# Depthwise taps as 64x64 matmuls, raw token rows, and norms after the gather, in a convolution and expert-choice kernel

## The chip, the cores and the metric

The kernel runs on one core of a Trainium2 chip. The core has a matrix engine (PE, with its weight loads shown apart as PEld), a vector engine (DVE), an activation engine (ACT), a general engine (POOL), a queue engine (SP), and 16 DMA engines. Each engine takes its instructions in order and waits on semaphores. The metric is the device time of one execution in microseconds: median 534.0 of three runs, 533.0 to 535.27. Below, "us" is microseconds and a line number such as L691 is a line of the kernel before.

## The reference

The input is 16 images of 128 channels and 28 x 28 positions. Two blocks follow each other, each added to its input.

```
h = LN over channels(x)                              # per position
h = relu(bn1(depthwise 3x3(h) + b)); a channel whose largest |h| is below 4.0 becomes 0
h = relu(bn2(pointwise 128x128(h) + b)); a channel whose largest |h| is below 0.001 becomes 0
x1 = x + h
t  = x1 as 12544 token rows of 128
n  = LN over a row(t)
logits = n @ Wr (8 experts); probs = softmax over all tokens
per expert: the 1024 tokens of largest prob; gelu(n[idx] @ W1 + b1) @ W2 + b2, times the prob
out = x1 + the sum of these rows, added at their tokens
```

## The kernel before, in words

**Stage 1, the images (until about 213 us).** `step(pair, u)` of each engine is one beat. In beat k the engines work on images k, k-1, ..., k-5 at once (`image(pair, u, lag)`); the middle of the beats is a hardware loop, the first and last are written out. For one image, in order:

- SP loads x. PE turns it (`turn_x`, L704, 7 transposes of 112 positions) into PSUM `psA`; DVE takes `bn_stats` of each token (L964), and a few small operations (`moments_a/b/c`, `inverse`, `shift`) with a square root on ACT (L463) between them make scale and shift. ACT norms the 7 tiles into `ln_tok` (L538), PE turns them back into `psB` (L769), and ACT copies them into the zero-padded `x_pad` (L570).
- The depthwise taps: PE does four of the nine, with a diagonal 128x128 weight each (`conv_half`, L691): two halves of 14 lines (392 columns), each half in a bank of its own of `psC`. DVE adds the other five: `first_tap` reads `psC` per half, then four `later_tap` over all 784 columns (L1009).
- ACT applies bn1 and relu (L519) and counts signs (L509). DVE turns the count into a 0/1 per channel and masks the pointwise weights (`mask_weights`, L1085). PE multiplies (L729), ACT applies bn2 and relu (L492) and counts signs (L500), DVE adds the masked result to x (`residual_sum`, L1103): this is x1, copied to `x1_all` by DMA.
- PE turns x1 into token rows in `psD` (L746) and computes the logits beside them (L750, 14 instructions). DVE takes the rows' statistics (L964), then the scaled logits (L1118, L1121). ACT norms the 7 tiles of 112 x 128 into `rows` (`norm_rows`, L483), and SP stores them in `token_rows`, 136 floats a token.

**Stage 2, the search (213 to 259 us).** DVE, ACT and PE find each expert's threshold in 16 rounds.

**Stage 3, the experts (259 to 462 us).** For each expert DVE finds the slots of its tokens (`slots_a` to `slots_d`, the index `slot_idx`). POOL gathers 1024 rows in 8 indirect DMAs (L403) and later adds the results to DRAM in 8 (L423, L426); `gather` and `scatter` of different experts stand in a fixed order on POOL. PE turns the gathered rows (`turn_picked`, L836), ACT copies them, PE does W1 (L857), ACT the gelu (L633), PE does W2 (L869), DVE adds the bias (L1302) and weighs (L1310). While the last expert runs, the sums of the first four experts are loaded, turned (`turn_first`, L923) and added to `x1_all` (`add_first`, L1343).

**Stage 4 (to the end).** The late sums are loaded, turned (L945), added and stored.

**The order by hand.** Every engine's order within a beat is written out. `turn_picked` waits only for its gather's DMA (L834). On DVE, `slots_*` of expert e+3 stand ahead of the bias and weighing of expert e.

Of the kernel before, what the change touches and what calls it, by code (L numbers as in the profile page):

```python
# [12 lines left out]
ds = bass.ds  # L13
# [11 lines left out]
ROW = C + E  # L25
# [3 lines left out]
HS = CAP // 2  # L29
DW_THRESH, PW_THRESH = 4.0, 0.001  # L30
# [5 lines left out]
PE_TAPS = 4  # L36
# [4 lines left out]
LOOP_FIRST, LOOP_END, LAST_PAIR = 3, B // 2 - 1, B // 2 + 3  # L41
# [37 lines left out]
def build(nc, x, dw_w, dw_b, bn1_g, bn1_b, bn1_m, bn1_v, pw_w, pw_b, bn2_g, bn2_b, bn2_m, bn2_v,  # L79
# [6 lines left out]
    with ExitStack() as ctx:  # L86
# [36 lines left out]
        zero_rows = sb("zero_rows", [P, TPI * C])  # L123
# [4 lines left out]
        tap_diag = sb("tap_diag", [128, PE_TAPS, 128])  # L128
# [72 lines left out]
        hid = sb("hid", [128, FT, CAP])  # L201
        y_sum = sb("y_sum", [128, SB, C])
# [13 lines left out]
        def ln_region(img):  # L216

            return row_tiles if isinstance(img, int) and img in (1, 3) else ln_tiles

        last_tiles = psC[0:P, :, :].rearrange("p a (t c) -> p (a t) c", c=C)  # L220

        def row_region(img):
            if isinstance(img, int) and img == B - 1:
                return last_tiles
            return ln_tiles if isinstance(img, int) and img == B - 3 else row_tiles
# [4 lines left out]
        def logit_region(img):  # L230
            return row_region(img)[:, TPI, 0:TPI * E].rearrange("p (t e) -> p t e", e=E)
# [14 lines left out]
        s_x1c = pair_of("x1_kept")  # L246
        s_t3, s_m3, s_std3, s_n3, s_rl = (sem(n) for n in (
            "row_tokens", "row_stats", "row_std", "row_normed", "row_logits"))
# [23 lines left out]
        s_pool, s_act = sem("pool_past_waits"), sem("act_past_waits")  # L272
# [9 lines left out]
        def _(sp):  # L282
# [6 lines left out]
            sp.dma_start(taps_w[:, :], dw_w.rearrange("c a h w -> c (a h w)")).then_inc(s_prm, 16)  # L289
            load_x(1, 1)  # L290

            def step(pair, u):
                on, img, q, use = image(pair, u, -2)
                if on:
                    sp.wait_ge(s_t1, img * 2 - 2)
                    load_x(img, q)
                on, img, q, use = image(pair, u, 2)
                if on:
# [3 lines left out]
                    if isinstance(img, int) and img == 0:  # L302
                        sp.wait_ge(s_const, 1)
                    sp.dma_start(y_t[:, ds(img, 1), :, :].rearrange("p i t c -> p (i t) c"),
                                 zero_rows[:, :].rearrange("p (t c) -> p t c", c=C)).then_inc(s_yz, 16)
                on, img, q, use = image(pair, u, 5)
                if on:
                    sp.wait_ge(s_rl, img + 1)
                    sp.wait_ge(s_n3, img + 1)
                    sp.dma_start(rows_t[:, ds(img, 1), :, :].rearrange("p i t c -> p (i t) c"),  # L310
                                 rows[:, q, :].rearrange("p (t c) -> p t c", c=ROW)).then_inc(s_rows[q], 16)
                on, img, q, use = image(pair, u, 3)
                if on:
                    sp.wait_ge(s_x1, img + 1)
                    sp.dma_start(x1_all[:, ds(img * HW, HW)], x1[:, q, :]).then_inc(s_x1c[q], 16)
# [12 lines left out]
            for img in range(B):  # L328
                sp.dma_start(late_t[:, ds(img, 1), :, :].rearrange("p i t c -> p (i t) c"),
                             zero_rows[:, :].rearrange("p (t c) -> p t c", c=C)).then_inc(s_lz, 16)  # L330
# [35 lines left out]
        def _(pool):  # L366
# [14 lines left out]
            nc.gpsimd.memset(zero_rows[:, :], 0.0)  # L381
# [73 lines left out]
        def _(act):  # L455
# [6 lines left out]
            def ln_root(img):  # L462
                nc.scalar.activation(ln_sm[:, 4, :], ln_sm[:, 3, :], ACT.Sqrt, bias=eps_c[0:P, :],  # L463
                                     scale=1.0 / C).then_inc(s_std1, 1)

            act.wait_ge(s_mom, 1)
            ln_root(0)
            act.wait_ge(s_bnv, 1)
            nc.scalar.activation(fold[:, 2:4], fold[:, 0:2], ACT.Sqrt).then_inc(s_bns, 1)

            def step(pair, u):
                onN, imgN, _, _ = image(pair, u, -1)
# [3 lines left out]
                on, img, q, use = image(pair, u, 0)  # L476

                def norm_rows():
                    act.wait_ge(s_sc, img5 + 6)
# [5 lines left out]
                    ins.then_inc(s_n3, 1)  # L485

                def second_activation():
# [9 lines left out]
                    if on2 and since(img2, 1):  # L497
                        act.wait_ge(s_sg1, img2)
# [4 lines left out]
                def first_signs():  # L503
                    if since(img2, 1):
                        act.wait_ge(s_kp1, img2)
                    if on3:
                        act.wait_ge(s_sg2, img3 + 1)
                    act.wait_ge(s_h1, img2 + 1)
# [14 lines left out]
                if ending and on3:  # L523
                    second_activation()
# [3 lines left out]
                if on5:  # L528
                    norm_rows()
# [868 lines left out]
```

## Time and profile before

| what | value |
|---|---|
| runs | 535.27, 533.0, 534.0 us; median 534.0 |
| span of the profiled execution | 502.9 us, 6936 instructions |
| median less span (what lies around the span) | 31.1 us |
| busy over the span | PE 361.9 us (72%), PEld 255.7 (51%), DVE 327.1 (65%), ACT 274.3 (55%), POOL 159.3 (32%) |
| granted TensorE clock, mean | 0.857 of full speed |

The profiled execution's time is told by its span, first to last instruction; what lies around it is taken as the difference to the median of the runs. Busy times are sums over the whole span, and the four stages have different limits. A row of the page's "busy tenths" shows this at a glance: each digit is one fortieth of the span (12.6 us).

```profile
PE   4989888888889985631021798999990498876575
DVE  5699988888889898578879548556620025235444
ACT  3577888888888876677640528556551240510000
POOL 4000000000000000000005777787888788876000
```

### The profile page before, as it was taken

Reading aid. Unit: us, or ns where it says so; the run is one execution under the profiler, and the core shown is the slowest. Engines: PE = TensorE matmul, PEld = TensorE weight load, DVE = VectorE, ACT = ScalarE, POOL = GpSimd, SP = SyncE. Lnnn points to the kernel's source line nnn. Section 1 sums busy time; section 2 is a strip of 40 time slices with the busy share of each in tenths; the row PEclk is TensorE's granted clock in tenths of the full one; section 3 lists DMA queues with packets and bytes.
Section 4 is the critical chain, followed back from the end, with each engine's and each line's share of the span. In section 5 each row is a group of like instructions: output and inputs, shape, how many; then the busy total and the mean of one; then the engine's idle time right before and its main releaser. Section 6 shows DMA issues by size and latency. Waiting matters only on the chain. (4 is left out here: it accounts for less than half of the span.)

```text
span 502.9 us, 6936 instructions
## 1 busy us (share of the span) xinstructions
PE 361.9 (72%) x1947; PEld 255.7 (51%) x1947; DVE 327.1 (65%) x1004; ACT 274.3 (55%) x587; POOL 159.3 (32%) x151
## 2 busy tenths in 40 slices
PE   4989888888889985631021798999990498876575
PEld 3656555566666553520011374677560467464453
DVE  5699988888889898578879548556620025235444
ACT  3577888888888876677640528556551240510000
POOL 4000000000000000000005777787888788876000
PEclk9999999999999997655555799999997598997755
DMA  4604555555554342479101223344443267847998
GB/s 103 188 38 141 185 168 185 167 185 168 185 182 150 130 131 96 137 238 392 71 1 33 55 56 94 95 65 64 83 85 34 55 189 134 194 61 169 285 390 344
DMA packets 36396, 72.01 MB, mean 143 GB/s; under 512 B 6385, under 2 KB 16785, under 8 KB 36369
## 3 DMA queue, kind: packets, MB, share of 16 engines
q1 hardware_dynamic: 24256, 56.52, 35.0%
q0 software_dynamic: 9472, 8.66, 11.2%
q10 hardware_dynamic: 2640, 6.51, 3.3%
q8 instruction: 12, 0.20, 0.2%
q14 instruction: 16, 0.12, 0.1%
HBM read 34.96 MB, written 30.29 MB: 130 GB/s over the span
## 5 line engine op out<-in xcount | busy, mean ns | idle before, releaser
L403 POOL DMA_INDIRECT picked<-token_rows,slot_idx x32 | 31.5, 986 | 270.7 <-issue 270.4
L691 PE MATMUL psC<-x_pad,tap_diag 128*128 128x392 f32 x256 | 90.8, 498 | 6.7 <-ACT x_pad L570 5.6
L1009 DVE SCALAR_TENSOR_TENSOR conv<-x_pad,taps_w,conv 128x784 f32<-128x784 f32 x64 | 65.9, 1030 | 0.8
L691 PEld LDWEIGHTS psC<-x_pad,tap_diag 128*128 128x128 f32 x256 | 46.1, 189 | 37.0 <-DVE conv L1009 5.1
L1302 DVE TENSOR_TENSOR y_sum<-psC,b_rows 128x512 f32<-128x512 f32 x15 | 10.4, 692 | 75.2 <-PE psC L869 75.2
L869 PE MATMUL psC<-w,hid 128*128 128x128 f32 x480 | 56.6, 280 | 2.2 <-ACT hid L633 2.1
L869 PEld LDWEIGHTS psC<-w,hid 128*128 128x128 f32 x480 | 55.8, 197 | 4.6 <-issue 3.0
L613 ACT ACTIVATE picked_T<-psA 128x512 f32<-128x512 f32 x16 | 9.0, 594 | 59.9 <-PE psA L836 59.9
L426 POOL DMA_INDIRECT moe_sum_late<-y_rows,slot_idx x24 | 37.9, 1581 | 9.5 <-issue 7.0
L483 ACT ACTIVATE rows<-psD,sm 112x128 f32<-112x128 f32 x98 | 35.7, 464 | 9.3 <-DVE sm L1001 9.3
L729 PE MATMUL psB<-act,pw_masked 128*128 128x392 f32 x64 | 27.9, 563 | 17.0 <-DVE pw_masked L1085 17.0
L426 POOL DMA_INDIRECT moe_sum<-y_rows,slot_idx x24 | 37.8, 1573 | 7.3 <-issue 7.0
L633 ACT ACTIVATE hid<-psB,b_T 128x512 f32<-128x512 f32 x32 | 21.7, 685 | 31.3 <-PE psB L857 31.3
L538 ACT ACTIVATE ln_tok<-psA,sm 112x128 f32<-112x128 f32 x98 | 36.0, 501 | 0.8 <-DVE sm L1001 0.8
L857 PE MATMUL psB<-picked_T,w 128*128 128x512 f32 x64 | 32.3, 629 | 4.9 <-ACT picked_T L613 3.9
L857 PE MATMUL psC<-picked_T,w 128*128 128x512 f32 x64 | 32.2, 614 | 0.0
L964 DVE BATCH_NORM_STATS2 st<-psD 112x6 f32<-112x128 f32 x112 | 24.8, 286 | 9.5 <-PE psD L750 7.9
L633 ACT ACTIVATE hid<-psC,b_T 128x512 f32<-128x512 f32 x32 | 21.8, 687 | 15.1 <-PE psC L857 15.1
L729 PEld LDWEIGHTS psB<-act,pw_masked 128*128 128x128 f32 x64 | 12.0, 206 | 31.0 <-DVE pw_masked L1085 19.1
L797 PE MATMUL psA<-sign_sum,half_same 128*128 128x4 f16 x16 | 3.0, 188 | 34.2 <-ACT x_in L585 33.2
L964 DVE BATCH_NORM_STATS2 st<-psA 112x6 f32<-112x128 f32 x105 | 22.2, 285 | 5.6 <-PE psA L704 5.6
L1199 DVE TENSOR_SCALAR_CACHE_REDUCE conv<-dist,cand 128x784 bf16<-128x784 f32 (+1 forms) x31 | 24.6, 830 | 0.9 <-DVE cand L1217 0.5
(211 smaller groups left out, 728.8 us busy)
## 6 DMA issues: line engine op xcount, KB each, us to landing
token_rows<-rows SPq DMA_DIRECT2D x16, 416.5 KB, 3.6
x_in<-in_x_dram SPq DMA_DIRECT2D x16, 392.0 KB, 3.5
x_res<-in_x_dram SPq DMA_DIRECT2D x16, 392.0 KB, 4.3
moe_sum<-zero_rows SPq DMA_DIRECT2D x16, 392.0 KB, 4.9
x_all<-x SPq DMA_DIRECT2D x16, 392.0 KB, 2.9
moe_sum_late<-zero_rows SPq DMA_DIRECT2D x16, 392.0 KB, 7.7
out_dram<-act ACTq DMA_DIRECT2D x16, 392.0 KB, 6.2
w<-in_L_ffn_W_dram SPq DMA_DIRECT2D x16, 256.0 KB, 3.3
```

The lines of the kernel that those rows point to most:

```text
L403: nc.gpsimd.indirect_dma_start(out=picked_in[k][:, b, :], out_offset=None, in_=rows_dram, in_offset=bass.IndirectOffsetOnAxis(ap=slot_idx[ ...
L426: nc.gpsimd.indirect_dma_start(out=sums, out_offset=at, in_=y_rows[:, q, b, :], in_offset=None, compute_op=ALU.add).then_inc(s_sca[q], 16)
L483: ins = nc.scalar.activation(rows[:, q5, t * ROW:t * ROW + C], row_region(img5)[:, t, :], ACT.Identity, bias=row_sm[:, 6, t:t + 1], scale= ...
L538: ins = nc.scalar.activation(ln_tok[:, q, t * C:(t + 1) * C], ln_region(img)[:, t, :], ACT.Identity, bias=ln_sm[:, 6, t:t + 1], scale=ln_s ...
L633: nc.scalar.activation(hid[:, f, h * HS:(h + 1) * HS], hidden_bank[f], ACT.Gelu, bias=b1_T[:, ds(e * FT + f, 1)]).then_inc(s_gelu, 1)
L691: ins = nc.tensor.matmul(psC[:, h, 0:HALF].rearrange("c (h w) -> c h w", w=W), tap_diag[:, n, :], x_pad_v[:, q, y0:y0 + LINES, dx:dx + W], ...
L729: nc.tensor.matmul(psB[:, h, 0:HALF], pw_masked[:, q, :], act1[:, q, h * HALF:(h + 1) * HALF], start=True, stop=True).then_inc(s_pw, 1)
L857: nc.tensor.matmul(hidden_bank[f], w1[:, q, f * 128:(f + 1) * 128], picked_T[:, h * HS:(h + 1) * HS], start=True, stop=True).then_inc(s_l1, 1)
L869: ins = nc.tensor.matmul((psA if first else psC)[:, h, b * C:(b + 1) * C], hid[:, f, lo:lo + 128], w2[:, q, f * C:(f + 1) * C], start=(f = ...
L964: ins = nc.vector.bn_stats(st[:, lo + t, :], region[:, t, :])
L1009: return nc.vector.scalar_tensor_tensor(o, x_pad_v[:, q, y0 + dy:y0 + dy + lines, dx:dx + W], taps_w[:, PE_TAPS + n:PE_TAPS + n + 1], acc, ...
L1199: return nc.vector.tensor_scalar(junk[:, column, 0:n], dist[:, 0:n], value.bitcast(F32), -offset, ALU.is_lt, ALU.add, accum_out=cnt[:, col ...
```

## The change

- **Taps.** PE takes seven taps, DVE two (`PE_TAPS = 7`). Each tap is now, for each half of the lines, two matmuls with 64x64 diagonal weights: channels 0 to 63 and 64 to 127. The upper half uses `x_pad` and writes its own 64 partitions (array quadrants (0,0) and (64,64)). For the lower half, SP copies 16 padded lines of `x_pad` by two DMAs of 64 partitions into `x_turned`, with the two groups of channels exchanged, so that its matmuls use the other two quadrants. Its weights are `tap_turned`. 28 matmuls an image, in the order n, half, row.
- **One more image in flight.** The copy needs a beat: images are at lags 0 to 6, not -1 to 5. The first tap of DVE waits for the whole convolution of the image, not for its half. The special regions for the first and last images are gone.
- **Token rows.** ACT copies the turned rows raw, in three instructions (4 tiles, 3 tiles, logits), DVE takes the statistics from the copy in SBUF, writes inverse and shift as columns 136 and 137 of each row (`ROW` is 138), and scales the logits there. Nothing norms the rows before they are stored.
- **After the gather.** `norm_picked(e, h)` on DVE norms the four gathered blocks of a half; `turn_picked` waits for it.
- **The rest.** `zero_rows` lies in `hid`, which ACT therefore doesn't use before the late sums are zeroed; the setup of the search is moved to a later beat; two more small loads of tap weights.

```diff
-ROW = C + E
+ROW = C + E + 2
-PE_TAPS = 4
+PE_TAPS = 7
@@ SP, in each beat
+                on, img, q, use = image(pair, u, 1)
+                if on:
+                    sp.wait_ge(s_pad, img * 2 + 2)
+                    for to, of in ((0, HC), (HC, 0)):
+                        sp.dma_start(x_turned[to:to + HC, q, :], x_pad[of:of + HC, q, LINES * PW:LINES * PW + LOWER])\
+                            .then_inc(s_xtu[q], 16)
@@ ACT, first in each beat
+                if on5:
+                    if since(img5, 2):
+                        act.wait_ge(s_rows[q5], use5 * 16)
+                    for a, tiles in enumerate(BANK_TILES):
+                        act.wait_ge(s_t3, img5 * 2 + a + 1)
+                        nc.scalar.activation(rows_v[:, q5, tiles.start:tiles.stop, 0:C], row_tiles[:, tiles.start:tiles.stop, :], ACT.Copy)
+                    nc.scalar.activation(rows_v[:, q5, :, C:C + E], row_logits, ACT.Copy).then_inc(s_n3, 1)
-                    for t in range(TPI):
-                        ins = nc.scalar.activation(rows[:, q5, t * ROW:t * ROW + C], row_region(img5)[:, t, :], ACT.Identity,
-                                                   bias=row_sm[:, 6, t:t + 1], scale=row_sm[:, 5, t:t + 1])
@@ ACT, before the experts
+            act.wait_ge(s_lz, 16 * B)
@@ PE, first in each beat
+            def conv_taps(img, q, use):
+                pe.wait_ge(s_pad, img * 2 + 2)
+                pe.wait_ge(s_xtu[q], use * 32 + 32)
...
+                for n in range(PE_TAPS):
+                    dy, dx = TAPS[n]
+                    for half, weights, lines in ((0, tap_diag, x_pad_v), (1, tap_turned, x_turned_v)):
+                        for row in range(2):
+                            of = slice(row * HC, row * HC + HC)
+                            col = row if half == 0 else 1 - row
+                            ins = nc.tensor.matmul(psC[col * HC:col * HC + HC, half, 0:HALF].rearrange("c (h w) -> c h w", w=W),
+                                                   weights[of, n, :], lines[of, q, dy:dy + LINES, dx:dx + W],
+                                                   start=(n == 0), stop=(n == PE_TAPS - 1))
+                ins.then_inc(s_conv, 1)
@@ PE, turn_picked
-                pe.wait_ge(s_gat[h][e % BUFS], e // BUFS * (8 * SB) + 8 * SB)
+                pe.wait_ge(s_pn, e * 2 + h + 1)
@@ DVE
+            def norm_picked(e, h):
+                k = e % BUFS
+                dve.wait_ge(s_gat[h][k], e // BUFS * (8 * SB) + 8 * SB)
+                for b in range(4 * h, 4 * h + 4):
+                    row = picked_in[k][:, b, :]
+                    ins = nc.vector.tensor_scalar(row[:, 0:C], row[:, 0:C], row[:, INV:INV + 1], row[:, SHIFT:SHIFT + 1],
+                                                  ALU.mult, ALU.add)
+                ins.then_inc(s_pn, 1)
...
+            norm_picked(0, 0)
+            slots_a(2)
+            slots_b(2)
+            norm_picked(0, 1)
...
             def expert(e, q, use, ahead):
+                if e < E - 2:
+                    norm_picked(e + 1, 0)
+                    norm_picked(e + 1, 1)
...
                 if e == E - 1:
...
-                    for img in range(7):
+                    for img in range(4):
                         add_first(img)
+                    norm_picked(e, 0)
+                    for img in range(4, 7):
+                        add_first(img)
+                    norm_picked(e, 1)
```

The new order in a beat is, on PE: taps of image k-2, turning back of k-1, pointwise of k-3, turning of k, rows and logits of k-4. On ACT: copy of k-5, roots, norm and pad of k-1, bn2 of k-3, bn1 of k-2. On DVE: mask of k-3, inverse and shift of k-1 and k-6, logits of k-6, statistics of k-5, two taps of k-2, statistics of k, residual of k-3, moments.

## Rows read from the trace of the kernel before

**Rows 1.** Busy time of each engine by stage (view by windows).
```profile
core 0: us, PE busy (x) PEld busy (x) DVE busy (x) ACT busy (x) POOL busy (x), PEclk, DMA share, GB/s
89.80:101.72 11.92, 10.65 (x57) 7.20 (x56) 10.62 (x35) 10.16 (x26) 0.00 (x0) 1.00 0.48 146
178.00:213.20 35.20, 22.84 (x112) 16.26 (x112) 27.05 (x100) 23.23 (x54) 0.00 (x0) 0.79 0.40 129
267.20:396.10 128.90, 94.09 (x538) 64.93 (x538) 64.06 (x182) 57.45 (x85) 101.77 (x90) 0.88 0.35 68
```

**Rows 2.** Timeline of ACT over one beat: start, us, operation, idle before.
```profile
97.88 2.55 ACT L483 ACTIVATE rows<-psD,sm 112x128 f32<-112x128 f32 x7 [0.87 <-DVE sm L1001]
100.29 2.58 ACT L538 ACTIVATE ln_tok<-psA,sm 112x128 f32<-112x128 f32 x7
104.13 0.95 ACT L500 ACTIVATE signs<-act,limits 128x784 bf16<-128x784 f32 x1
105.08 1.02 ACT L519 ACTIVATE act<-conv,fold 128x784 f32<-128x784 f32 x1
109.84 2.55 ACT L483 ACTIVATE rows<-psD,sm 112x128 f32<-112x128 f32 x7 [0.91 <-DVE sm L1001]
```

**Rows 3.** Timeline of PE and PEld in the same beat.
```profile
101.43 1.45 PE L750 MATMUL psD<-wr_c,x 128*112 128x8 f32 x14
102.73 0.95 PE L704 MATMUL psA<-ident,x_in 128*112 128x128 f32 x7
103.42 2.28 PEld L691 LDWEIGHTS psC<-x_pad,tap_diag 128*128 128x128 f32 x8
103.52 2.80 PE L691 MATMUL psC<-x_pad,tap_diag 128*128 128x392 f32 x8
106.16 0.84 PE L769 MATMUL psB<-ident,ln_tok 112*128 112x112 f32 x7
111.32 1.58 PE L729 MATMUL psB<-act,pw_masked 128*128 128x392 f32 x4 [1.00 <-DVE pw_masked L1085]
```

**Rows 4.** Groups by line over 0 to 190 us: count, busy us, mean ns.
```profile
L1009 DVE SCALAR_TENSOR_TENSOR conv<-x_pad,taps_w,conv 128x784 f32<-128x784 f32 x60 | 61.8, 1030 | 0.7
L1009 DVE SCALAR_TENSOR_TENSOR conv<-x_pad,taps_w,psC 128x392 f32<-128x392 f32 x32 | 19.7, 617 | 2.7 <-PE psC L691 2.7
```

**Rows 5.** Timeline of ACT and DVE: the pads of images 0, 5, 15; the last logits.
```profile
12.89 0.95 ACT L570 ACTIVATE x_pad<-psB 128x448 f32<-128x448 f32 x2 [1.44 <-PE psB L769]
58.94 0.89 ACT L570 ACTIVATE x_pad<-psB 128x448 f32<-128x448 f32 x2 [0.72 <-PE psB L769]
177.44 0.89 ACT L570 ACTIVATE x_pad<-psB 128x448 f32<-128x448 f32 x2
213.16 0.22 DVE L1118 TENSOR_TENSOR logits<-psC,sm 112x56 f32<-112x56 f32 x1
```

**Rows 6.** DMA issues over the span: KB each, median us to landing.
```profile
x_all<-x SPq DMA_DIRECT2D x16, 392.0 KB, 2.9
prm<-in_L_conv_dw_b_dram SPq DMA_DIRECT2D x1, 0.5 KB, 2.0
```

**Rows 7.** Timeline of the first expert's start, on DVE, PE, ACT and POOL.
```profile
275.35 0.27 DVE L1249 TENSOR_SCALAR s_d<-logits_T,bc 112x112 f32<-112x112 f32 x1
277.63 0.34 DVE L1263 TENSOR_SCALAR s_tie<-s_run,s_ahead,bc 112x112 f32<-112x112 f32 x1
277.26 1.09 PE L836 MATMUL psA<-ident,picked 128*128 128x128 f32 x4
278.45 0.60 ACT L613 ACTIVATE picked_T<-psA 128x512 f32<-128x512 f32 x1 [19.31 <-PE psA L836]
286.45 0.95 POOL L403 DMA_INDIRECT picked<-token_rows,slot_idx  x1 [0.30 <-DVE slot_idx L1290]
```

**Rows 8.** Timeline, later experts: where PE and POOL wait.
```profile
396.12 1.12 PE L836 MATMUL psA<-ident,x_in 128*128 128x128 f32 x4 [18.29 <-DMA x_in<-token_rows,slot_idx]
426.30 1.07 DVE L1343 TENSOR_TENSOR x_all<-psD,x_all 128x448 f32<-128x448 f32 x2 [0.72 <-PE psD L923]
426.61 1.01 PE L836 MATMUL psA<-ident,x_res 128*128 128x128 f32 x4
435.22 1.04 DVE L1343 TENSOR_TENSOR x_all<-psD,x_all 128x448 f32<-128x448 f32 x2 [0.34 <-PE psD L923]
435.31 0.60 PE L836 MATMUL psA<-ident,x_res 128*128 128x128 f32 x4
447.68 1.55 POOL L426 DMA_INDIRECT moe_sum_late<-y_rows,slot_idx  x1 [2.50 <-DVE y_rows L1310]
```

More of the change, by code:

```diff
@@ L304, in step @@
                     sp.dma_start(y_t[:, ds(img, 1), :, :].rearrange("p i t c -> p (i t) c"),
[L305 to L315, printed above, removed]
+                                 zero_rows.rearrange("p (t c) -> p t c", c=C)).then_inc(s_yz, 16)
             steps(sp, step)
@@ L460, in _ @@
             nc.scalar.activation(warm[:, :], eps_c[:, :], ACT.Sqrt)
[L462 to L469, printed above, removed]
             def step(pair, u):
-                onN, imgN, _, _ = image(pair, u, -1)
+                k = pair * 2 + u
+                on1, img1, q1, _ = image(pair, u, 1)
                 on2, img2, q2, _ = image(pair, u, 2)
@@ new lines, in step @@
+                if on6:
+                    nc.scalar.activation(row_sm[:, 4, :], row_sm[:, 3, :], ACT.Sqrt, bias=eps_t[0:P, :],
+                                         scale=1.0 / C).then_inc(s_std3, 1)
+                if isinstance(img1, int) and img1 == 0:
+                    act.wait_ge(s_bnv, 1)
+                    nc.scalar.activation(fold[:, 2:4], fold[:, 0:2], ACT.Sqrt).then_inc(s_bns, 1)
+                if on1:
+                    act.wait_ge(s_sc, k)
+                    if since(img1, 2):
+                        act.wait_ge(s_t2, img1 * 2 - 2)
+                    for tiles in BANK_TILES:
+                        for t in tiles:
+                            ins = nc.scalar.activation(ln_tok[:, q1, t * C:(t + 1) * C], ln_tiles[:, t, :], ACT.Identity,
+                                                       bias=ln_sm[:, 6, t:t + 1], scale=ln_sm[:, 5, t:t + 1])
+                        ins.then_inc(s_n1, 1)
@@ new lines, in step @@
+                if isinstance(img1, int) and img1 == 0:
+                    act.wait_ge(s_wps, 1)
+                    nc.scalar.activation(pw_T[:, :], psD[:, 0, 0:128], ACT.Copy)
+                    nc.scalar.activation(b1_T[:, :], psD[:, 0, 128:128 + E * FT], ACT.Copy).then_inc(s_wsb, 1)
+                if on1:
+                    if isinstance(img1, int) and img1 == 0:
+                        act.wait_ge(s_const, 1)
+                    if since(img1, 2):
+                        act.wait_ge(s_tap, img1 - 1)
+                        act.wait_ge(s_xtu[q1], image(pair, u, 1)[3] * 32)
+                    for a, (lo, n) in enumerate(((0, 16), (16, 12))):
+                        act.wait_ge(s_t2, img1 * 2 + a + 1)
+                        nc.scalar.activation(x_pad_v[:, q1, 1 + lo:1 + lo + n, 1:1 + W],
+                                             psB[:, a, 0:n * W].rearrange("c (h w) -> c h w", w=W), ACT.Copy).then_inc(s_pad, 1)
@@ L572, in step @@
-                if on:
-                    roots()
-                if on2 and not ending:
-                    first_signs()
+                    if since(img2, 1):
+                        act.wait_ge(s_kp1, img2)
+                        act.wait_ge(s_sg2, img2)
+                    act.wait_ge(s_h1, img2 + 1)
+                    nc.scalar.activation(signs[:, :], act1[:, q2, :], ACT.Sign, bias=limits[:, 0:1],
+                                         accum_out=keep1[:, 0:1]).then_inc(s_sg1, 1)
```

407 lines of the change are left out of this document (162 added, 245 removed).

## The prediction

> **What bounds the kernel now.** I read the stages first (view by windows), then one beat of the image stage engine by engine (timeline), then the chain of waits after 372 us. In the image stage a beat takes 11.92 us, and PE is busy 10.65 of it, DVE 10.62, ACT 10.16 [rows 1]: no engine has room. DVE binds by a little, since short dependent operations on it leave gaps between them that count as idle but can't be filled. ACT waits 0.87 to 0.91 us a beat for DVE's shift and for little else [rows 2]. The pads start at 12.89 (image 0), 58.94 (image 5) and 177.44 (image 15): 11.85 us an image from 5 to 15, and then 35.7 us until the last logits at 213.16 [rows 5]. The search (46 us) is not touched. In the expert stage POOL is busy 101.77 of 128.90 us in 90 instructions [rows 1]; with the 0.30 us before each, 27 us more, it never pauses, and PE stands 18.29 us until the gather of expert 6 lands [rows 8]. So up to 396 us POOL's order binds, and after it the chain through PE, DVE's `add_first` and the last expert, until POOL waits 2.50 us for `y_rows` at 447.68 [rows 8]. The sum is made against the profiled span, 502.9 us; 31.1 us lie around it up to the median 534.0, and I hold them fixed.
>
> **The change, DVE and ACT in a beat.** Of five taps DVE keeps two halves of 0.617 and one full of 1.03, so it loses three full taps: 3 x 1.03 = 3.1 us [rows 4]. A copy of inverse and shift adds about 0.2. Its beat falls from about 11.7 to 8.8 us. ACT loses seven norms, 2.55 us [rows 2]. It gains copies of 512, 384 and 56 elements. The pair of the ACT copies of 512 elements isn't there, but one is 0.60 [rows 7]; with overlap like that of the seven norms (2.55 for 7 of 0.46 each) I take 0.49 + 0.37 + 0.20 = 1.06 us. Bounds: 0.8 (pure elements at the rate of the 784-element relu, 1.02 [rows 2]) and 1.4 (no overlap). ACT's beat is then: copies 1.06, two roots 0.4, wait for inverse and shift 0.65, norms 2.45, wait for PE's turning 0.3, pad 0.85, wait for the pointwise 0.55, bn2 1.35, signs 0.94, relu 1.03, signs 0.95: 10.5 us.
>
> **PE in a beat.** The taps cost now 16 instructions (4 taps, 2 halves, 2 passes of an fp32 matmul) in 5.7 us: eight in 2.80, less the overhang of the last, 0.33 us each [rows 3]. After, there are 7 x 4 x 2 = 56 of the same 392 columns. If the four quadrants stream together that is 14 x 0.33 = 4.6 us; if two do, 28 x 0.33 = 9.2; if none, 18.5. The trace has no small tile, so these are the bounds. I take 4.6 to 4.9, since the four matmuls of a tap name four different quadrants, and two neighbours in the order share neither rows nor columns. Around them I put 0.2 us each, as a matmul's own length less its spacing (0.49 less 0.33), for the array to run empty when it goes from the whole to quarters and back; the bounds are 0 and 0.4. The rest is 0.66 (turn back), 1.4 (pointwise), 0.7 (turn), 0.67 + 1.45 (rows, logits) [rows 3], and about 0.5 of waits for ACT's pad, which now stands between two of PE's steps: 10.4 to 10.6 us. So PE and ACT end level, and a beat is 10.55 us (10.3 to 11.2).
>
> The Trainium skill (TensorE: Matmul & The Clock Gate, Part 3, The mechanism) says that a weight load overlaps a running matmul only where its group of rows differs. The trace disagrees: eight loads on all 128 rows take 2.28 us inside the 2.80 us of their own eight matmuls [rows 3]. By the rule every second load would stand in the open; by the row none does, and my sum has none.
>
> **The image stage.** Steady: 10 x (11.85 - 10.55) = 13.0 us won (6.5 to 15.5 by the range of a beat). Filling: before, images 0 to 5 take 46.05 us to the pad of image 5. After, each early beat runs pad, two issues of the copy and its landing (0.9 + 2.6), taps 5.0, turn back 0.85, pad 0.9: 10.3 us, five times 51.3, with the last two a bit longer: 51.6, which is 5.6 us lost. The copy's landing is not in the trace; 0.5 KB land in 2.0 us and 392 KB in 2.9 [rows 6], two transfers of 123 KB between, and up to 3.5 beside the loads of the beat. In the steady part the copy has about 4 us before PE comes to it, so it hides. Draining: a beat more, but shorter ones; the taps are 3 us shorter for the last image, DVE's chain too, the store of image 13's rows (landing near 4 us) must be back before ACT copies those of 15, and the halves are no longer overlapped. I take 35.2 us against 35.7 (33 to 38). Sum: -13.0 + 5.6 - 0.5 = -7.9 us, to 205 us.
>
> **The experts.** `norm_picked` is four operations of two scalars each. The nearest row is 0.34 us alone, spaced 0.26, at 112 columns [rows 7]; for 128 I take 0.29, so 1.15 us a half with its semaphore; bounds 0.8 and 1.5. It lies on the path in four places:
> - Expert 0: between slots of expert 1 (end 275.35) and of expert 2. The turning at 277.26 and the rank matmuls behind it go 1.2 later, and POOL takes the index of expert 2 exactly when it is ready (0.30 from DVE) [rows 7], so its whole chain moves: +1.2.
> - Experts 1 to 4: two halves ahead of `slots_a` hold PE's tie matmul some 2 us each. PE has 18.29 us in hand at expert 6 [rows 8]: 0, up to four times 2 us fit.
> - Expert 6: gather lands, norm, then turning: +1.2.
> - Expert 7: PE turned at 426.61 while DVE added until 427.37; now it waits for the add and the norm: +1.9. The same at 435.31 with the add until 436.26: +2.0 [rows 8].
>
> Together +6.3 us (4.3 to 8.5); POOL's wait of 2.50 us before `y_rows` at 447.68 shows that nothing takes it back. ACT's wait for the zeroed late sums lies in the search, where SP issues them, so it costs nothing. The two added loads delay image 1 by 0.9 us, which the filling holds. Wider rows are 1.5% more bytes: nothing.
>
> **Sum.** 534.0 - 7.9 + 6.3 = 532.4; I say 532. The likeliest case's own range is 525 to 541.
>
> **Rivals.**
> 1. *Two passes in order.* An fp32 matmul is two instructions on one quadrant. If matmuls start in program order, the second pass of one waits for its first, and only the next matmul's first pass runs beside it: 28 x 0.33 = 9.2 us, what seven whole taps would cost. PE's beat becomes 15.1 us and binds from the first beat. The last logits come near 277 us, 64 later, plus 6.3: 604 (598 to 611). For it: 256 instructions for 128 matmuls, each the full 0.33. Against: nothing here shows how quadrants share. It decides from where the taps cost over 6 us. The Trainium skill (TensorE: Matmul & The Clock Gate, Part 3, The mechanism) says matmuls start and end strictly in order; no run here shows it for tiles. It gives this case.
> 2. *The copy lands late.* With the zeroing, the residual load and the row store on the same DMA engines, busy 0.48 of a beat [rows 1], it lands after 3.5 us or more and PE waits each beat: 11.1 to 11.6 us, filling 3 us longer: 540 to 548.
> 3. *More is hidden.* Norms at 0.8 us a half (-1.6), a copy of 2.0 us (-3), a beat of 10.3 (-2.5), shorter drain: 524 to 527.
> 4. *It doesn't do what it says*: quadrants one at a time, 18.5 us: a beat of 25, about 750.
>
> **Chances.** Forecast 0.42, rival 1 0.25, rival 2 0.10, rival 3 0.20, rival 4 0.03. No change means within 0.5% (531.3 to 536.7), about what a measurement of this kernel can tell. Faster is rival 3 with 0.16 of the forecast: 0.36. Same is 0.19 of the forecast. Slower is the rest, 0.45. The range must reach into rival 1: 520 to 606 leaves out rival 4, half of rival 1 and a few hundredths below.
>
> **What would show it.** The taps: spacing of 56 instructions an image, 4.6 to 5 us from first to last, or over 9. The beat: pads 10.3 to 10.7 us apart, ACT and PE waiting under 1 us each for the other. The pad of image 5 near 64.5 us, of image 15 near 170, the last logits near 205. Copies of 1.06 us on ACT. In the experts: four norms in 1.15 us, PE waiting for DVE at experts 6 and 7, POOL still the bound up to about 390. I am wrong if PE's wait before the taps is for the copy in each beat, if the experts' path grows by under 4 us, or if the taps exceed 6 us.

## The result, and the profile after

The kernel after takes 535.6 us (median of 20 runs, 533.1 to 541.3), the kernel before 532.8 us in the runs beside them: a ratio of 1.0052, 95% interval 1.0029 to 1.0074. It is slower by half a per cent, where the prediction said 0.4% faster. The time lies in the range, the direction does not. The chances gave "slower" 0.45, but 0.38 of that stood for slow taps or a late copy, and neither came. A median here is of all runs of a kernel, a ratio with its interval of those within 1.5% of its fastest.

**First, the profile to compare with.** The listed spans of the kernel after are 1.8 us below their times. So the 31.1 us that the prediction put around the span of before do not exist: its profiled execution, 502.9 us, was some 28 us shorter than all its timed runs. Before was therefore profiled again, unchanged (its spans here: 529.0 to 534.4). First the spans, again and after (granted clock behind them):

```profile
core 0: 531.6 us, clock 0.832
```

```profile
core 0: 538.8 us, clock 0.812
```

The two profiles of before agree up to the first gather (267.15 and 267.89 us) and behind the last expert. They differ between. PE's timeline of before, again, over the first experts and at expert 6:

```profile
286.49 0.60 PE L836 MATMUL psA<-ident,picked 128*128 128x128 f32 x4
301.63 3.78 PE L857 MATMUL psB<-picked_T,w 128*128 128x512 f32 x4 [14.54 <-ACT picked_T L613]
...
342.90 0.37 PE L869 MATMUL psC<-w,hid 128*128 128x128 f32 x1 [1.72 <-issue]
344.98 0.37 PE L869 MATMUL psC<-w,hid 128*128 128x128 f32 x1 [1.72 <-issue]
...
416.58 1.12 PE L836 MATMUL psA<-ident,x_in 128*128 128x128 f32 x4 [7.10 <-DMA x_in<-token_rows,slot_idx]
```

PE stands 14.5 us where it stood 2.4, and later, from 333 to 346 us, starts one matmul each 0.7 to 2.1 us, with no releaser. I call this a crawl. From the first gather to the first `y_rows` of expert 6 the profile again takes 27.5 us longer, nearly all of the 28.7 us between the two spans. A crawl is in every later profile of either kernel, and there is none in [rows 7] and [rows 8]. The reader's second look goes to the last row: PE's time in hand at expert 6 is 7.10 us, not 18.29 [rows 8].

**The image stage after.** A beat by windows, ACT and PE in it. The trace calls `x_turned` by the name `hid`, in whose memory it lies:

```profile
99.08:109.77 10.69, 10.21 (x95) 6.76 (x95) 7.81 (x31) 9.28 (x23) 0.00 (x0) 1.00 0.71 223
```

```profile
94.55 0.96 ACT L482 ACTIVATE rows<-psD 112x512 f32<-112x512 f32 x2
95.40 0.22 ACT L483 ACTIVATE rows<-psD 112x56 f32<-112x56 f32 x1
...
96.66 2.56 ACT L501 ACTIVATE ln_tok<-psA,sm 112x128 f32<-112x128 f32 x7 [0.67 <-DVE sm L966]
```

```profile
93.43 0.55 PE L673 MATMUL psC<-x_pad,tap_diag 64*64 64x392 f32 x2
93.44 0.55 PE L673 MATMUL psC<-hid,tap_turned 64*64 64x392 f32 x2
...
97.76 0.49 PE L673 MATMUL psC<-x_pad,tap_diag 64*64 64x392 f32 x2
97.77 0.49 PE L673 MATMUL psC<-hid,tap_turned 64*64 64x392 f32 x2
98.22 0.60 PE L691 MATMUL psB<-ident,ln_tok 112*128 112x112 f32 x4
...
104.36 0.55 PE L673 MATMUL psC<-x_pad,tap_diag 64*64 64x392 f32 x2 [0.25 <-DMA hid<-x_pad]
```

Each pair of rows is four quadrant matmuls, whose rows start 0.01 us apart; the pairs follow each other by 0.33 us, 14 of them, so 56 instructions take 4.8 us where 16 took 5.7 [rows 3]. DVE falls from 10.62 to 7.81 us a beat, PE and ACT end level, a beat is 10.65 us on average of ten. Pads and last logits, against [rows 5]:

```profile
12.26 0.57 ACT L517 ACTIVATE x_pad<-psB 128x448 f32<-128x448 f32 x1
67.13 0.58 ACT L517 ACTIVATE x_pad<-psB 128x448 f32<-128x448 f32 x1
173.63 0.58 ACT L517 ACTIVATE x_pad<-psB 128x448 f32<-128x448 f32 x1
203.64 0.21 DVE L1071 TENSOR_TENSOR logits<-rows,sm 112x56 f32<-112x56 f32 x1
```

The copy lands in 2.3 us (DMA issues, as [rows 6]):

```profile
hid<-x_pad SPq DMA_DIRECT2D x32, 120.0 KB, 2.3
```

**The expert stage after.** Where POOL waits, which in [rows 7] and [rows 8] it did only once:

```profile
258.50 1.16 POOL L411 DMA_INDIRECT picked<-token_rows,slot_idx  x1 [252.55 <-issue]
...
302.04 0.99 POOL L431 DMA_INDIRECT moe_sum<-y_rows,slot_idx  x1 [13.04 <-DVE y_rows L1257]
...
432.86 1.64 POOL L434 DMA_INDIRECT moe_sum_late<-y_rows,slot_idx  x1 [9.46 <-DVE y_rows L1257]
...
483.82 1.55 POOL L434 DMA_INDIRECT moe_sum_late<-y_rows,slot_idx  x1 [15.56 <-DVE y_rows L1257]
```

The waits at 302, 433 and 484 us are not all the change's: before, again, has 13.44, 4.10 and 6.17 us at these places. PE's waits for DVE: the ties of experts 4 to 7 (the matmul L779 counts the tokens at the threshold, which `slots_a` and `slots_b` need), and the last expert's turnings:

```profile
314.03 0.33 PE L779 MATMUL psD<-s_run,before 112*112 112x2 f32 x2 [2.77 <-DVE s_run L1188]
346.65 0.43 PE L779 MATMUL psD<-s_run,before 112*112 112x2 f32 x2 [2.66 <-DVE s_run L1188]
373.71 0.51 PE L779 MATMUL psD<-s_run,before 112*112 112x2 f32 x2 [9.59 <-DVE s_run L1188]
393.99 0.33 PE L779 MATMUL psD<-s_run,before 112*112 112x2 f32 x2 [2.64 <-DVE s_run L1188]
...
456.69 1.11 PE L795 MATMUL psA<-ident,x_res 128*128 128x128 f32 x4 [1.84 <-DVE x_res L1230]
458.54 3.75 PE L816 MATMUL psB<-picked_T,w 128*128 128x512 f32 x4 [0.73 <-issue]
...
469.63 1.12 PE L795 MATMUL psA<-ident,x_res 128*128 128x128 f32 x4 [1.87 <-DVE x_res L1230]
471.43 3.78 PE L816 MATMUL psB<-picked_T,w 128*128 128x512 f32 x4 [0.69 <-ACT picked_T L585]
```

Before, again, the tie waits are under 0.8 us each. So the image stage gave back 9 us by the first gather, and the stages behind it took more than that.

### The profile page after: what moved, and what is told of

It reads as the page before. It is cut to its first block, busy times and chain, and to the rows that moved or that the text cites. A ratio compares the mean times of both kernels' runs of the same rounds, so it can differ in the third digit from the quotient of the medians.

```text
span 538.8 us, 8090 instructions
## 1 busy us (share of the span) xinstructions
PE 377.4 (70%) x2587; PEld 254.9 (47%) x2587; DVE 303.0 (56%) x1035; ACT 255.7 (47%) x523; POOL 159.6 (30%) x151
## 4 chain that ended last, share of the span: by engine, by line
PE 41%; ACT 21%; DVE 14%; issue 12%; DMA 5%; another core or an unknown queue 4%; SPq 1%; ACTq 1%; DVEq 0%
PE psC L828 11%; ACT ln_tok L501 6%; PE psB L816 5%; PE psC L816 5%; PE psC L673 4%; PE psB L703 4%; DMA x_pad<-moe_sum_late 3%; ACT act L524 2%; ACT act L540 2%; PE psD L882 2%; DVE x_all L1295 2%; ACT rows L482 2%; PE psB L691 2%; ACT x_in L557 1%
## 5 line engine op out<-in xcount | busy, mean ns | idle before, releaser
L673 PE MATMUL psC<-x_pad,tap_diag 64*64 64x392 f32 x448 | 81.7, 514 | 7.2 <-DMA hid<-x_pad 4.0
L673 PE MATMUL psC<-hid,tap_turned 64*64 64x392 f32 x448 | 81.7, 514 | 0.0
L828 PE MATMUL psC<-w,hid 128*128 128x128 f32 x480 | 62.1, 289 | 14.7 <-issue 8.1
L673 PEld LDWEIGHTS psC<-x_pad,tap_diag 64*64 64x64 f32 x448 | 33.3, 139 | 43.6 <-issue 36.3
L816 PE MATMUL psB<-picked_T,w 128*128 128x512 f32 x64 | 40.1, 759 | 18.2 <-ACT picked_T L585 15.1
L501 ACT ACTIVATE ln_tok<-psA,sm 112x128 f32<-112x128 f32 x112 | 40.9, 466 | 9.3 <-DVE sm L966 9.3
L816 PE MATMUL psC<-picked_T,w 128*128 128x512 f32 x64 | 35.5, 665 | 1.8 <-ACT hid L605 1.7
L816 PEld LDWEIGHTS psB<-picked_T,w 128*128 128x128 f32 x64 | 14.7, 246 | 35.8 <-issue 19.8
L673 PEld LDWEIGHTS psC<-hid,tap_turned 64*64 64x64 f32 x448 | 31.2, 139 | 0.0
L974 DVE SCALAR_TENSOR_TENSOR conv<-x_pad,taps_w,psC 128x392 f32<-128x392 f32 x32 | 18.5, 619 | 16.8 <-PE psC L673 16.0
L524 ACT ACTIVATE act<-psB,fold 128x392 f32<-128x392 f32 x32 | 21.0, 678 | 10.9 <-PE psB L703 10.9
```

Of the source, the lines that this page charges most:

```text
L501: ins = nc.scalar.activation(ln_tok[:, q1, t * C:(t + 1) * C], ln_tiles[:, t, :], ACT.Identity, bias=ln_sm[:, 6, t:t + 1], scale=ln_sm[:, ...
L524: nc.scalar.activation(act2[:, q3, h * HALF:(h + 1) * HALF], psB[:, h, 0:HALF], ACT.Relu, bias=fold[:, 9:10], scale=fold[:, 5:6]).then_inc ...
L673: ins = nc.tensor.matmul(psC[col * HC:col * HC + HC, half, 0:HALF].rearrange("c (h w) -> c h w", w=W), weights[of, n, :], lines[of, q, dy: ...
L816: nc.tensor.matmul(hidden_bank[f], w1[:, q, f * 128:(f + 1) * 128], picked_T[:, h * HS:(h + 1) * HS], start=True, stop=True).then_inc(s_l1, 1)
L828: ins = nc.tensor.matmul((psA if first else psC)[:, h, b * C:(b + 1) * C], hid[:, f, lo:lo + 128], w2[:, q, f * C:(f + 1) * C], start=(f = ...
L974: return nc.vector.scalar_tensor_tensor(o, x_pad_v[:, q, y0 + dy:y0 + dy + lines, dx:dx + W], taps_w[:, PE_TAPS + n:PE_TAPS + n + 1], acc, ...
```

## The experiments

Each kernel was timed in turns with the kernel before. As the runs of a kernel spread by 3 to 14 us, I compare medians, and write the difference to the median of before in the same session.

| kernel | median us | against before | ratio, 95% |
|---|---|---|---|
| before again | 532.9 | +0.5 | 0.996 to 1.001 |
| after again | 535.4 | +3.0 | 1.003 to 1.010 |
| norms' operations out | 526.4 | -6.0 | 0.985 to 0.995 |
| norms out whole | 524.5 | -8.0 | 0.975 to 0.986 |
| norms behind the ties | 535.1 | +1.4 | 0.996 to 1.003 |
| norms out for expert 7 | 532.4 | -1.3 | 0.980 to 0.990 |
| norms for expert 7 alone | 533.8 | +0.6 | 0.994 to 1.001 |
| norms on GpSimd, rows | 532.6 | -1.1 | 0.996 to 1.003 |
| before plus norms | 545.0 | +11.3 | 1.014 to 1.024 |
| row norms on DVE, late store | 627.7 | +94.6 | 1.176 to 1.185 |
| row norms on DVE, early | 533.5 | -1.3 | 0.992 to 0.999 |
| norm order changed | 529.6 | -3.5 | 0.988 to 0.994 |
| the same, again | 533.1 | -1.7 | 0.989 to 0.997 |
| before, gather 2 held | 532.3 | -0.8 | 0.998 to 1.001 |
| after, gather 5 held | 541.1 | +6.4 | 1.007 to 1.018 |

**1 and 2. Both kernels again**, no edit.

> The kernel before, unchanged. The profiled execution of before spans 502.9 us, yet all its timed runs lie at 530 to 537, and the kernel after, whose own profiled execution spans 538.8, has spans only 1.8 us below its times. Theory A (the prediction's): about 31 us lie outside the span, so this profile shows a span near 503 again and the listed spans of before are near 503. Theory B: the span of before is usually near 530 and the profile of before shows a lucky execution without some 27 us of stalls in the expert stage; then this profile shows a span of 528 to 532, with POOL idle somewhere between 300 and 440 us, where it never paused before.

> The kernel after, unchanged. Its profile shows PE standing or issuing one matmul each 2.1 us at 278 to 292, 321 to 335, 361 to 368 and 417 to 426 us, some 40 us in all, and no row names a releaser. Theory 1: chance of that one execution; the stalls are elsewhere or gone here and the span falls to 505 to 515 (the time to 533 by what lies around it). Theory 2: they belong to every execution, for instance because PE waits for its instructions: the same four places again within 5 us, span 532 to 540. Ratio to before 1.005 by the earlier runs.

Theory B holds for before. For after, theory 2 holds as to the places: its second profile has the crawls there again, though with a span of 527.8, under the range given. That PE waits for its instructions no run tests. The transfers speak against one form of it: in the DMA view, instruction transfers have queues of their own, and none runs from 284 to 302 us of before, again, nor in any of the four stretches named for after, so none of these crawls ends with one.

**3 and 4. The norms out of the expert stage.**

```
 def norm_picked(e, h):
     dve.wait_ge(s_gat[h][k], ...)        # 4: out as well, PE waits for s_gat
-    for b in range(4 * h, 4 * h + 4):
-        nc.vector.tensor_scalar(row..., INV, SHIFT, ALU.mult, ALU.add)
```

> norm_picked keeps its wait for the gather and its signal, but its four operations are left out (picked rows stay unnormed). It prices the 64 operations themselves. By the prediction's step they are 1.15 us a half on the path in four places, so 4.6 us less than after: 531. If DVE's order matters at experts 1 to 4 as well (two halves ahead of slots_a hold PE 2.2 us each there), 10 to 13 us less: 523 to 526. If PE's standing without releaser sets the stage, under 2 us less.

> norm_picked is left out whole (picked rows stay unnormed) and PE waits for the gather itself, as before: the expert stage is that of before, fed by the new image stage. By the prediction's steps the whole 6.3 us go: 529. If DVE's wait for the gather ahead of the slots and of the bias is what costs (the wait, not the operations), it is 5 us or more under the run that keeps the wait. If the image stage's 8.7 us (first gather at 258.5 against 267.2) reach the end, it comes out 8 to 9 us under before: ratio 0.984.

Without the norms the rows stay unnormed. The operations cost 9.0 us, above the 4.6 of the prediction's step and near the 10 to 13 forecast if DVE's order matters; the wait costs 2.0 more, which lies within the spread of these six runs each. What is left, -8.0 us, is the image half by itself; the prediction had -7.9.

**5. The other half by itself:** before, with `norm_picked` at the places of after.

> The kernel before with norm_picked alone added, at the places it has after, on rows already normed (a second scaling by two columns of the row, so its values are not the reference's; the work is the same): the expert half of the change without the image half. By the prediction's step: +6.3 us, 538.7. By the runs that took the norm out of after (535.4 against 524.5): +9 to +11 us, 541 to 544. If the two halves only interact (nothing alone): 533.

+11.3 us, against 11.0 by taking it out of after (535.4 - 524.5): nearly twice the 6.3 of the prediction, both ways. That the two agree to 0.3 us is luck: by the ratios of the table they are 10.0 and 13.6. PE's tie waits are again 2.75, 2.79, 10.35 and 2.64 us.

**6 and 7. Which experts.**

```
 def norm_picked(e, h):
+    if e == E - 1:      # 7: if e < E - 1
+        dve.sem_inc(s_pn, 1); return
```

> The four operations of norm_picked are left out for expert 7 alone (its picked rows stay unnormed); the waits stay. The prediction gave expert 7 3.9 us, and the traces show 34.5 to 36.7 us from the first y_rows of expert 6 to the first of expert 7, against 28.8 before: if this is the norms' and the adds' order, the distance falls to about 32.4 and the time by 3 to 4 us, to 532; the rest of the 9 us of the norms' price then lies in the experts before. If the last expert carries it all: 527.

> The mirror of the kernel that leaves the norm out for expert 7: its operations stand for expert 7 alone and are left out for experts 0 to 6 (those rows stay unnormed); the waits stay. If the two shares add up (9.1 us for all operations, 3 for the last expert by its mirror), experts 0 to 6 carry 6 us and this is 529 to 530. If the prediction's zero for experts 1 to 4 holds and only its 1.2 + 1.2 fall away: 533.

By the first, expert 7 costs 4.3 us (+3.0 to -1.3) and experts 0 to 6 the other 4.7. By its mirror, 6.6 (-6.0 to +0.6) and 2.4. So the shares add up only roughly: 4.3 to 6.6 for the last expert, 2.4 to 4.7 for the operations before it. Even this is loose: the first kernel's twelve runs go from 521.7 to 535.6, and its ratio, 0.980 to 0.990, would put it 6 to 11 us below before, where the medians say 1.3. Neither forecast of the mirror was met: 529 to 530 was too low, and 533 fits by number but its reason, a last expert of 3.9, does not. From the first `y_rows` of expert 6 to that of expert 7 it takes 28.8 us in both profiles of before and without the last norms (30.3 and 32.4 with none at all), 35.5 to 36.8 with them. Two stands of 1.9 us explain half. Most of the other half goes with PE's clock: by windows over the first half's turning and four first-layer matmuls, after, and the kernel without the last norms:

```profile
456.60:464.00 7.40, 6.58 (x12) 3.09 (x13) 0.03 (x1) 2.38 (x4) 6.18 (x5) 0.58 0.65 101
```

```profile
452.30:457.60 5.30, 4.44 (x16) 2.27 (x16) 0.80 (x2) 2.66 (x4) 4.38 (x4) 1.00 0.90 198
```

PE stood 1.84 us, and the granted clock of the stretch is 0.58 instead of 1.00 (mostly the 1.2 GHz level instead of 2.4): four matmuls take 3.75 us instead of 1.96, and again 3.78 after the second stand. That the stand brought the clock down is not shown. In this profile it was low before the first stand: the last `turn_first` ahead of it took 1.54 us instead of 0.86. Before, again, has the same there, without a stand, and is back at speed for the first layer:

```profile
453.31 1.54 PE L882 MATMUL psD<-ident,x_pad 112*128 112x112 f32 x7 [0.42 <-DVE x_all L1295]
```

```profile
453.52 1.54 PE L923 MATMUL psD<-ident,x_pad 112*128 112x112 f32 x7 [0.25 <-DVE x_all L1343]
456.65 1.95 PE L857 MATMUL psB<-picked_T,w 128*128 128x512 f32 x4 [0.73 <-issue]
```

With the norms out whole, and so without a stand, the first four matmuls still take 3.62 us; behind the second turning they take 1.98. In the kernel without the last norms it is the other way round, 1.96 and 3.48. So behind the first turning the low clock comes without a stand too. Behind the second it goes with the stand: in all six profiles in which PE stands 1.87 us there the four matmuls take 3.78 us, in the others 1.98, except the 3.48 above and 3.38 in one more.

**8 to 10. Order on DVE**, the second kernel run twice.

```
 def expert(e, ...):
-    norm_picked(e + 1, 0); norm_picked(e + 1, 1)
     slots_a(e + 3); slots_b(e + 3)
+    norm_picked(e + 1, 0); norm_picked(e + 1, 1)
     slots_c(e + 3); slots_d(e + 3)
```

and, in the second kernel only, for the last expert

```
-    for img in range(4): add_first(img)
     norm_picked(e, 0)
-    for img in range(4, 7): add_first(img)
+    for img in range(6): add_first(img)
     norm_picked(e, 1)
+    add_first(6)
```

> In the loop over experts norm_picked(e+1) stands behind slots_b(e+3) instead of ahead of slots_a(e+3); nothing else moves. Theory 1, DVE's order is the price at experts 1 to 4: PE's wait for the tie matmul's input falls back from 2.6 to 2.8 us each to about 0.4, 9 us of PE's time in four places, of which the 7 us that PE has in hand are given back first: 529 to 533. Theory 2, only the operations count, wherever they stand, or PE's standing without a named releaser sets the stage: 534 to 536, as after.

> after, with DVE's order alone changed: norm_picked(e+1) behind slots_b(e+3), and in the last expert the first half's norm ahead of all adds and the second half's ahead of the last add. Theory 1, order: from the first y_rows of expert 6 to that of expert 7 falls from 35 to 37 us to 32 to 33, on top of what the first move gave: 530 to 532. Theory 2, the last expert's length is set by the matmuls' lower clock behind PE's pause and not by where the norms stand: 35 us stay and the time is that of the first move, 534 to 535.

> The kernel with DVE's order changed, again, beside other kernels: seven runs gave 525.7 to 535.1 with a median of 529.6, a ratio of 0.991 to before. If that holds: 528 to 532 and a ratio under 0.996. If it was chance: 533 to 535, as the first move alone gave.

The first move takes 1.6 us off (+3.0 to +1.4); two of the four tie waits fall to 0.8 us and less, the third is still 4.5. The time, 535.1, is what the second theory gave, and the intervals of it and after touch, so this is weak. Both moves give -3.5 and -1.7, below before both times: 33.9 and 33.5 us between experts 6 and 7, and PE's second turning waits 0.48 us. The second run of it kept the ratio forecast (0.993, under 0.996), but its 533.1 us lies where chance was to put it. Its interval is below 1 both times, by 0.3 to 0.7% in the medians; it is the version that is fastest against before with all the work done. The four matmuls behind the first turning are slow here as well (3.75 us), though PE doesn't stand.

**11 and 12. What the crawl is.** In before, GpSimd's gather of expert 2 is held until PE has done the first layer of expert 0 (`pool.wait_ge(s_l1, 2 * FT)`); in after, its gather of expert 5 until PE has done the second layer of expert 2 (`pool.wait_ge(s_l2, 6)`).

> The kernel before; GpSimd issues the gathers of expert 2 only once PE has run all eight first-layer matmuls of expert 0. It tests the 13 us in which PE stands or crawls behind the first turning of expert 0 in every repeated execution (285 to 301 us), which the profile shown of before lacks. Theory 1, PE crawls while GpSimd issues indirect DMAs: PE is free at about 290 instead of 301, and the time falls by 5 to 11 us, to 522 to 528. Theory 2, the crawl has another cause (instructions, clock): PE crawls as long as before, the gathers come 13 us later and expert 2 may wait for them: 532 to 540.

> after, with GpSimd's gather for expert 5 held until PE has done the second layer of expert 2. In all three traces with the norms in the loop the two halves of y_rows of expert 2 lie 7.2 to 10.8 us apart, 3.6 in all without, and this gather starts within 1 us of those matmuls. Theory 1: PE crawls because GpSimd issues indirect DMAs while it runs short matmuls, and the norms moved PE's work onto the gather: the two halves come 3.6 to 4.5 us apart, and PE's wait of 6.6 to 9.6 us for the tie of expert 6 falls to about 2.7. GpSimd gives the hold back later, so the time is 532 to 537. Theory 2: the distance comes from something else in the norms' kernels: it stays at 7 us or more.

With gather 2 held, GpSimd's last gather before the hold ends at 287.3 us, and (PE's timeline)

```profile
285.52 0.60 PE L839 MATMUL psA<-ident,picked 128*128 128x128 f32 x4
290.96 3.62 PE L860 MATMUL psB<-picked_T,w 128*128 128x512 f32 x4 [4.84 <-ACT picked_T L616]
```

PE is free 10.7 us earlier than in the unheld kernel, as the first theory had it. But once the gathers start again at 300.99, PE crawls again, its second layer of expert 1 starting 10.1 us late at 335.83, 4 us behind the last gather of that burst. The time doesn't move, where the first theory forecast 522 to 528: the crawl is put off, not saved. With gather 5 held, the two halves of `y_sum` of expert 2 on DVE:

```profile
356.97 0.69 DVE L1251 TENSOR_TENSOR y_sum<-psC,b_rows 128x512 f32<-128x512 f32 x1 [3.42 <-PE psC L830]
...
360.54 0.69 DVE L1251 TENSOR_TENSOR y_sum<-psC,b_rows 128x512 f32<-128x512 f32 x1 [2.10 <-PE psC L830]
```

The unheld kernel has them at 358.01 and 368.59, the second after a wait of 9.11 us. 3.6 us apart, and a tie wait of 2.44 us instead of 9.59: theory 1 on both counts. The hold costs more than expected, 541.1 us for 532 to 537: GpSimd stands 8.81 us for it and PE then 7.54 us at expert 6. So the third crawl needs the gather running beside that matmul group; that it is the delayed chain that brings the two together is my reading, which fits that without a hold the seven profiles without norm operations at experts 1 to 4 have 3.6 us there, and the seven with them 7.2 to 10.8.

**13 to 15. The image half with normed rows.** GpSimd norms a row tile in SBUF before its store (13); or DVE does, behind its taps, with the store at the end of SP's step (14); or DVE does, ahead of the row statistics, with the store first in SP's step (15). All three have experts without norms.

```
+ for t in range(TPI):      # 13: nc.gpsimd, and the store behind the on-chip copy
+     nc.vector.tensor_scalar(row, row, row_sm[:, 5, t:t + 1], row_sm[:, 6, t:t + 1], ALU.mult, ALU.add)
```

> The new image stage with normed rows: GpSimd, idle there, norms each image's rows in SBUF (7 operations of 112x128) before SP stores them, the store stands behind the on-chip copy on SP, and the expert stage has no norm and waits for the gather as before. Theory 1: the norm on DVE was the only price of the expert stage and GpSimd's work hides in a beat of 10.6 us: first gather near 257, time 524 to 526, ratio 0.984. Theory 2: GpSimd and VectorE share what they read SBUF through, so DVE's taps stretch: a beat of 11 us or more, 529 to 533. Theory 3: GpSimd takes over 1.5 us an operation, 10.5 a beat: beat 11 to 12, about 535.

> The new image stage, but token rows stored normed: DVE norms each image's rows in SBUF behind its taps (7 operations of 112x128, about 1.9 us a beat), where it stands 1.15 us for PE's turning and where its moments are ready 0.9 us before ACT takes them; SP stores them at the end of its step; rows are narrow again and the expert stage has no norm. Theory 1: those gaps hold the norms, the beat stays at 10.6 us, first gather near 257 to 259, and the time is that of the kernel with the norm left out: 524 to 527. Theory 2: the norms push ACT's root, so the beat is 11.2 us or more as with GpSimd's norms (10.9, 11.65, 10.6), and the time 530 to 533.

> The mended form of the run whose store came too late (627.7 us: ACT's copy stood 6.8 us a beat for the store of the image two before, which stood at the end of SP's step). DVE norms the rows ahead of the next image's row statistics, straight behind inverse and shift, and SP stores them at the start of its step as after does; rows are narrow, the expert stage has no norm. Theory 1: the store lands ahead of ACT's next copy (issue near 98.8, landing 4 us, copy near 105), the 1.9 us fit into DVE's 1.15 us stand and its 0.9 us in hand, beat 10.6 to 10.8: 525 to 529. Theory 2: DVE's chain to ACT's relu grows by the 1.9 us and the beat with it, 11.5 us or more: 534 to 540.

The late store was a mistake of mine, outside both theories: ACT copies the next image into the same buffer one beat after the norm, not two (ACT's timeline):

```profile
116.60 0.98 ACT L481 ACTIVATE rows<-psD 112x512 f32<-112x512 f32 x2 [6.83 <-DMA token_rows<-rows]
```

ACT waits 6 to 8 us a beat, the granted clock is 0.76 (from 100 to 140 us), and it costs 95 us in all. With the early store the beat is 10.6 us as forecast:

```profile
96.90:107.50 10.60, 10.21 (x95) 6.77 (x95) 9.57 (x38) 9.19 (x23) 0.00 (x0) 1.00 0.73 224
```

DVE's norms fit in (9.57 us busy), but the time is 533.5, not 525 to 529. In its profile the last image's logits are 3.5 us later than in after and the first gather comes at 261.1. That can't be weighed from one profile: the ten profiles with after's image stage have their first gather anywhere from 256.4 to 262.7. So what separates this kernel from the one with the norms out, 6.7 us, stays open, and the runs were in another session. With GpSimd's norms (3.76 us for 7, against DVE's 1.88) the store stands behind the copy. Most beats are still 10.5 to 10.9 us, two are 11.5 and 11.7, and draining takes 37.1 us for after's 30.0, with ACT waiting 3.54 and 7.09 us for a store. The first gather comes at 266.3, nearly all of the image half lost; the slower norm and the later store were not tried apart, and so none of the three theories is shown.

## Why the prediction was wrong

**What bounds the kernel** was right for the image stage. For the expert stage "POOL's order binds" and "PE has 18.29 us in hand" were read from one execution that lacked 27 us of crawl. The number that should have warned was on the same page as the times: 31.1 us around a span had nothing to fill them.

**DVE and ACT in a beat.** Copies 0.96 and 0.22 us, 1.07 from first to last, for 1.06; wait 0.67 for 0.65. DVE is busy 7.81 us in the beat, 2.8 less than before, for 2.9 forecast; 8.8 counted its gaps.

**PE in a beat.** 4.8 us from first start to last end, for 4.6 to 4.9; a beat 10.65 for 10.55. One reason given for it was wrong: of two neighbours in the order n, half, row every second pair shares its columns, and all four quadrants ran together all the same. Rival 1 and rival 4 fall with the first pair of rows. The in-order rule of the Trainium skill (TensorE: Matmul & The Clock Gate, Part 3, The mechanism) would have had the quadrants' second passes in the way. The starts 0.01 us apart and 14 slots for 56 passes show that it does not bind across quadrants, if the two passes of a matmul stand next to each other in the program; the records don't name the pass. Rival 2, a late copy: PE's wait for it is there in a beat, but 0.25 us long, landing 2.3 us.

**The image stage.** Images 5 to 15 took 106.5 us for 105.5 forecast (before 118.5). Filling cost 8.2 us (5.9 in the second pair of profiles) for 5.6. Draining took 30.0 us (31.5) for 35.2; that DVE's and PE's shorter chains count at the end too is the likely reason, not a tested one. These errors cancel in part: -9.5 us at the last logits (-11.2), -8.7 at the first gather (-10.3), for -7.9. The -8.0 in time is the same number by luck: in the profile without the norms the first gather comes 11.1 us ahead of before, again, and some of it is lost behind that.

**The experts: +6.3 us was the step that failed.** Measured 11.0 and 11.3, outside its bounds of 4.3 to 8.5. The four operations themselves were right:

```profile
266.70 1.11 DVE L1230 TENSOR_SCALAR picked<-picked 128x128 f32<-128x128 f32 x4
```

1.11 us for 1.15. What failed was where they count:

- *Experts 1 to 4 at 0.* The hold on PE was seen ("some 2 us each") and set against 18.29 us in hand. In the second profile of before, whose span agrees with the timed runs, there are 7.1. Four holds, each 2.2 us longer than before's 0.4, make some 9, and at expert 6's tie PE waits 6.8 us more still (4.1 in the second profile of after), beside GpSimd's gather of expert 5. From the second `y_rows` of expert 0 to the first of expert 6 it takes 129.0 us in before again and with the norms out, and 133.1 and 138.6 in after: 4 to 10 us for 1.2. In time, part of this is made up elsewhere: all before expert 7 comes to 4.4 to 6.7 us (the operations' 2.4 to 4.7 and the wait's 2.0) for 2.4.
- *Experts 0 and 6 at 1.2 each.* Neither is there in this form. GpSimd's first 24 gathers take 30.5 us in after and 30.4 in before again, so its chain did not move: 0.30 is the spacing of all its gathers and told nothing of when the index was ready. And PE turns expert 6's rows at 418.56 us without a wait, as its delayed chain comes there behind the gather: all its time in hand is used up.
- *Expert 7 at 3.9.* 4.3 to 6.6 us. The two waits have the size forecast (1.84 and 1.87); the lower clock behind each, 1.8 us on the first four matmuls alone, was not in the sum. Only the second goes with a stand in all profiles.

Net +3.0 for -1.6. The prediction's own sign of error, "if the experts' path grows by under 4 us", looked only the other way: it asked what would make the norms cheaper and gave no condition for 11.

## What to carry to other kernels

Time in hand that hides an edit must be read from an execution whose span agrees with the timed runs; where it doesn't, look for the missing time before counting on any cover. Work moved onto an in-order engine ahead of what another engine waits for holds the other at every round, even if its own operand is ready (here 2.7 us instead of 0.4): put it behind the step that the others need. And where PE is made to stand, look at its granted clock behind the stand in a trace, not at the stand alone.

## What was not expected of the hardware

- PE crawls while GpSimd issues gathers back to back (0.95 us each, 0.30 between): its matmuls start 0.7, 1.4 or 2.1 us apart and others see its results 3 to 14 us late, until 2.6 to 4.4 us behind the last gather. Holding gathers moves the crawl (301.6 to 291.0 us) and leaves the time where it was (532.3 us). Which resource the two share stays open, and so does why one execution of before was free of it, at the same order of gathers; so the gathers alone don't bring it.
- Four 64x64 fp32 matmuls on four quadrants, two passes each, take the 0.33 us per pass of one whole-array matmul.
- Seven of GpSimd's tensor_scalar of 112x128 take 3.76 us, 0.54 each, twice DVE's 0.27, and 3.03 us while the stage drains and DVE does less. In the beat looked at, one of DVE's taps took 1.18 us beside it instead of 1.03.
